# Starting the second expert layer on three tiles after nine of ten row tiles, with late scatters on their own semaphores

## The chip, the cores and the metric

The kernel runs on one core of a Trainium2 chip. A core has a matrix engine (TensorE, PE in the rows), a vector engine (VectorE, DVE), a scalar engine (ScalarE, ACT), GpSimd (POOL) and SyncE (SP), which here only issues DMAs and waits. The engines run their own instruction streams in order and meet at semaphores. The metric is the device time of one execution in microseconds (us), lower is better. The chip grants TensorE a clock at one of two levels, 2.4 or 1.2 GHz; the rows show it as a share, 1.00 or 0.50.

## What is computed

Two layers, each a graph part and a mixture-of-experts part, over 1250 rows of 512 numbers and 20000 edges. What matters here is the end of the second layer, cut from the reference:

```python
    # second graph layer (x: 1250 x 512)
    h = agg * jax.lax.rsqrt(deg_in)[:, None]
    h = h @ W + b
    h = (h - mu) * jax.lax.rsqrt(var + LN_EPS) * gamma + beta
    x = x + gelu(h)
    # second expert layer: one of six experts for each row
    probs = softmax(layernorm(x) @ w_gating)
    gate1 = max(probs);  gate2 = second(probs);  gate1 = gate1 / (gate1 + gate2 + EPS)
    hidden = gelu(layernorm(x) * gamma @ w1[expert])      # 512 -> 256
    x = x + gate1 * (hidden @ w2[expert])                 # 256 -> 512
```

Which expert takes a row is known only when its gating product is there, so rows have to be sorted by expert at run time.

## The kernel before

The 1250 rows are ten row tiles of 125. The end of the program, from 748 us of the profiled execution, runs like this.

**Graph part, per row tile j.** TensorE finishes four column blocks of the last aggregation piece (`aggregate_rest`, L853, ten matmuls of 250 columns each) and multiplies by W (`project(j)`, L880, four matmuls of 512 columns). VectorE adds the bias (`add_bias`, L2040), takes statistics (`hidden_stats`, L2046), centres, shifts (`centre_rows`, L2053; `shift_rows`, L2060), ScalarE does the gelu, VectorE adds it to x (`add_layer`, L2066) and takes statistics again (`layer_stats`, L1540).

**Routing, per row tile i.** TensorE transposes the tile (`turn_unit`, L893), multiplies by the gating weights (`route_unit`, L903) and ranks the rows in their experts (`rank_unit`, L910, one small matmul). VectorE copies the logits (`take_logits1`, L2076), finds the largest and its index (`best_of`, `index_of`, `number_of`), makes the one-hot mask (`mask_of`, L2096) that the ranking needs, and turns ranks into slots (`take_slots`, L2103 to L2106). Running counts pass from tile to tile, so the tiles are ranked in order. ScalarE writes the normalised rows (`unit_rows`) and GpSimd scatters them to their slots in memory (`scatter_unit`, L1454), an area of 1280 slots for each expert. All ten scatters add to one semaphore, `rows1_out`. SyncE meanwhile stores x to `x_d` (L301), from which it is gathered later.

**Hand-over.** After the tenth tile TensorE takes out the counts (L958) and VectorE works out, for 15 tiles of 128 slots, the expert and the first slot (`take_counts`, L1798 to L1814; `slot1_made`). VectorE then scales the logits (L2233, L2235), ScalarE takes their exponential (L1267), VectorE makes the gate of every row (L2238 to L2245; `gate1_made`), and SyncE writes the gates beside the rows in `x_d` (two small DMAs, L301).

**Expert tiles, t = 0 to 14.** SyncE loads a tile from the slots (`load_rows1`, L459); the first three after `slot1_made` and all ten scatters, the others when a buffer is free. Between the third and the fourth load stands the wait for `gate1_made` with the write of the gates. TensorE transposes the rows (`turn_rows1`, L766, ×4), does the hidden product (L759, four matmuls of 256 columns), transposes the hidden rows (`turn_hidden`, L766, ×2) and does the output product (L759, two matmuls of 512 columns). ScalarE moves the transposes (L1272, L1282) and does the gelu (L1277). GpSimd gathers x and the gate of the tile's rows from `x_d` (`gather_kept`, L1492), which needs every store to `x_d` (`x_kept`), the gates among them. VectorE adds gate × product to x (`add_kept`, L2259; `yy_moved`), and GpSimd scatters the result to the output (L1499). `output_product(t)` writes one of two banks and waits for `yy_moved` of tile t - 2.

The order of all these steps on each engine is written out by hand in the source. In the first expert layer the same hand-over exists in two steps already: its first 6 tiles are known after 7 row tiles (`EARLY_TILES`, `EARLY_ROWS`).

Of the kernel before, what the change touches and what calls it, by code (L numbers as in the profile page):

```python
# [39 lines left out]
AHEAD = 3  # L40
E0, H0, K0 = 8, 256, 2
# [5 lines left out]
EARLY_TILES, EARLY_ROWS = 6, 7  # L47
assert K0 * P * EARLY_ROWS - E0 * (TM - 1) > (EARLY_TILES - 1) * TM
assert E == EP * ET and N == P * T and MT0 % LANES == 0
# [40 lines left out]
def gnn_moe_kernel(nc, x, src, dst, L0_gnn_W, L0_ffn_gate_w, L0_ffn_w1, L0_ffn_w2, L0_ffn_w3,  # L90
# [7 lines left out]
    with ExitStack() as ctx:  # L98
# [159 lines left out]
        rows_in = [sem(f"rows_in{k}") for k in range(T)]  # L258
# [14 lines left out]
        SCATTERED0 = [16 * K0 * len(range(k, T, 3)) for k in range(3)]  # L273

        @block.sync
        def _(sp):
# [140 lines left out]
            for t in range(3, MT0 + 2):  # L417
                if t == EARLY_TILES - 1:
                    sp.wait_ge(S("slot_made"), 3)
                    for k in range(3):  # L420
                        sp.wait_ge(rows_out[k], 16 * K0 * len(range(k, T, 3)))
# [14 lines left out]
            sp.wait_ge(rows_in[4], 16 * K0)  # L436
            move(CS_C, counts_d[2 * C * P:N, :].rearrange("(i p) d -> p i d", p=P), S("counts_in2"))
            sp.wait_ge(rows_in[T - 1], 16 * K0)
# [4 lines left out]
            for e in range(E1):  # L443
                sp.dma_start(W1B[:, e, :].rearrange("p (c n) -> p c n", c=C),
                             L1_ffn_w1[e].rearrange("(c p) n -> p c n", c=C)).then_inc(S("w1b_in"), 16)
            sp.wait_ge(S("agg_made"), C * len(AGGREGATED))
# [3 lines left out]
            for i in range(T):  # L450
                sp.wait_ge(S("xn_made"), 2 * T + i + 1)
                move(x_d[P * i:P * i + P, 0:D], X[:, i, :], S("x_kept"))
# [8 lines left out]
            sp.wait_ge(S("rows1_out"), 16 * T)  # L461
            for t in range(3):
                load_rows1(t)
# [9 lines left out]
        def _(pe):  # L473
# [433 lines left out]
            def rank_unit(i):  # L907
# [3 lines left out]
                  .then_inc(S("rank1_made"), 1)  # L911
            project(0)
# [3 lines left out]
            aggregate_rest(0, 0)  # L916
            aggregate_rest(0, 1)
            project(4)
            project(5)
            turn_unit(0)  # L920
            aggregate_rest(0, 2)
            project(6)
            aggregate_rest(0, 3)
            project(7)
            project(8)
            route_unit(0)
            turn_unit(1)
            turn_unit(2)
            route_unit(1)
            rank_unit(0)  # L930
            turn_unit(3)
            route_unit(2)
            rank_unit(1)
            route_unit(3)
            project(9)
            rank_unit(2)
            turn_unit(4)
            turn_unit(5)
            route_unit(4)
            turn_unit(6)  # L940
            rank_unit(3)
            route_unit(5)
            turn_unit(7)
            route_unit(6)
            rank_unit(4)
            route_unit(7)
            rank_unit(5)
            turn_unit(8)
            turn_unit(9)
            rank_unit(6)  # L950
            route_unit(8)
            rank_unit(7)
            route_unit(9)
            rank_unit(8)
            rank_unit(9)

            pe.wait_ge(S("slot1_ready"), T)
            pe.matmul(bank(6, 1, 8), ident[0:126, 125:126], counted[:, T % 2, :], start=True, stop=True)\  # L958
              .then_inc(S("count_made"), 1)
            pe.wait_ge(S("slot1_made"), 1)  # L960
            pe.wait_ge(S("xg_made"), C)
            pe.wait_ge(S("w2b_in"), 16 * E1)
# [3 lines left out]
            def turn_rows1(t):  # L966
                expert1[t] = pe.value_load(owner_i[0:1, t:t + 1], min_val=0, max_val=E1 - 1)
# [4 lines left out]
            def hidden_product(t):  # L972
                pe.wait_ge(S("z_moved"), t + 1)
# [8 lines left out]
            def output_product(t):  # L982
                pe.wait_ge(S("gg_moved"), t + 1)
                above_zero(pe, S("yy_moved"), t - 1)
                product(6 + t % 2, act1T[t % 2], W2B, expert1[t], 2, D).then_inc(S("yy_made"), 1)

            turn_rows1(0)
            for t in range(MT1 + 1):
                if t >= 1:
                    turn_hidden(t - 1)  # L990
# [4 lines left out]
                if t >= 1:  # L995
                    output_product(t - 1)
# [3 lines left out]
        def _(act):  # L1000
# [227 lines left out]
            for n in range(AT_ONCE):  # L1228
                for c in range(C):
                    move_aggregate(n, c)  # L1230
# [1063 lines left out]
```

## Time and profile before

| | |
|---|---|
| median of 3 runs | 912.6 us (912.29 to 912.64) |
| the profiled execution | 913.43 us, its span 911.7 us |
| TensorE busy | 837.7 us, 92% of the span |
| VectorE busy | 568.0 us, 62% |
| ScalarE busy | 375.9 us, 41% |
| GpSimd busy | 205.0 us, 22% |
| mean granted TensorE clock | 0.968 |

The span is the profiled stretch; the execution's own time is 1.73 us more. TensorE is busy nearly throughout, with two holes: one at 663 to 678 us, between the layers, and one at 826 to 838 us, at the hand-over to the second expert layer. This change works on the second.

### The profile page before, as it was taken

How to read it: one execution, taken by the hardware profiler on the slowest of the kernel's cores; microseconds unless marked ns; L12 is line 12 of the kernel's file. 1: busy time of each engine (PE TensorE's matmuls, PEld its weight loads, DVE VectorE, ACT ScalarE, POOL GpSimd, SP SyncE). 2: the span in 40 equal slices, each digit the busy share in tenths (PEclk: the TensorE clock that was granted, in tenths of full speed). 3: DMA queues.
4: the chain of work that ended last, by engine and by line, in shares of the span. 5: the costliest groups of instructions: out<-in, count | busy, mean ns of one | idle time of the engine just before them, and what ended most of it. 6: DMA issues, size and time to landing. Idle time of an engine off the chain costs nothing.

```text
span 911.7 us, 15969 instructions
## 1 busy us (share of the span) xinstructions
PE 837.7 (92%) x5074; PEld 564.6 (62%) x5074; DVE 568.0 (62%) x1880; ACT 375.9 (41%) x680; POOL 205.0 (22%) x376
## 2 busy tenths in 40 slices
PE   6999999999999999999999799999829999993996
PEld 3456555457777777777777667777514446672664
DVE  6389999357777788778777365555544406873111
ACT  1234434456566666566556334343300023341331
POOL 4100000000022012101212512222154502562443
PEclk9999999999999999999999999999969999975999
DMA  9818888796102223110924545554135340364550
GB/s 258 314 28 207 201 209 211 120 341 169 30 25 70 65 76 83 38 43 25 303 72 140 206 123 162 178 166 151 59 87 139 96 146 1 112 196 103 159 171 28
DMA packets 87363, 121.01 MB, mean 133 GB/s; under 512 B 40781, under 2 KB 50157, under 8 KB 87021
## 3 DMA queue, kind: packets, MB, share of 16 engines
q1 hardware_dynamic: 73677, 101.82, 39.1%
q0 software_dynamic: 13600, 18.11, 7.1%
q8 instruction: 46, 0.75, 0.4%
q14 instruction: 40, 0.33, 0.1%
HBM read 65.52 MB, written 57.08 MB: 134 GB/s over the span
## 4 chain that ended last, share of the span: by engine, by line
PE 74%; DVE 13%; DMA 4%; issue 3%; POOL 2%; ACT 2%; SPq 0%; DVEq 0%; POOLq 0%; ACTq 0%
PE ps L759 17%; PE ps L649 10%; PE ps L678 10%; PE ps L853 9%; PE ps L660 8%; PE ps L539 4%; PE ps L880 4%; DVE R_B L1633 4%; PE ps L766 3%; DVE R_B L1632 2%; PE ps L544 2%; DVE R_A L1734 1%; PE ps L489 1%; PE ps L715 1%; DVE R_B L1628 1%
## 5 line engine op out<-in xcount | busy, mean ns | idle before, releaser
L759 PE MATMUL ps<-R_B,R_A 128*128 x612 | 185.9, 445 | 2.9 <-ACT R_A L1272 1.1
L759 PEld LDWEIGHTS ps<-R_B,R_A 128*128 128x128 f32 x612 | 111.4, 193 | 34.8 <-issue 24.8
L1104 ACT ACTIVATE R_A<-R_A,neg_max 125x1250 f32<-125x1250 f32 x80 | 106.6, 1333 | 57.1 <-DVE neg_max L1734 57.1
L1734 DVE CUSTOM_DVE_ANT_0 R_A<-ps,R_B,neg_max 125x417 f32<-125x417 f32 (+1 forms) x160 | 97.7, 649 | 29.0 <-PE ps L649 29.0
L649 PE MATMUL ps<-R_B 64*125 64x417 f32 (+1 forms) x480 | 106.5, 544 | 2.1 <-ACT XN L1046 1.5
L678 PEld LDWEIGHTS ps<-R_W,XN 125*64 125x64 f32 x1600 | 85.3, 136 | 23.9 <-issue 23.8
L660 PE MATMUL ps<-ident,R_A 125*125 125x125 f32 x800 | 98.7, 278 | 0.0
L660 PEld LDWEIGHTS ps<-ident,R_A 125*125 125x125 f32 x800 | 94.9, 188 | 1.5 <-DVE R_W L1741 0.7
L678 PE MATMUL ps<-R_W,XN 125*64 125x125 f32 x1600 | 94.7, 272 | 0.8 <-DVE counted L1791 0.8
L1111 ACT ACTIVATE R_W<-ps 125x500 f32<-125x500 f32 x120 | 66.1, 585 | 51.2 <-PE ps L660 51.2
L1633 DVE TENSOR_SCALAR R_B<-R_B 125x418 bf16<-125x418 uint16 x200 | 77.7, 389 | 0.0
L1734 DVE CUSTOM_DVE_ANT_0 R_A<-ps,R_B 125x417 f32<-125x417 f32 x80 | 44.2, 591 | 45.4 <-PE ps L649 32.1
L539 PE MATMUL ps<-XT,R_W 128*128 128x500 f32 (+1 forms) x192 | 70.9, 513 | 0.7 <-ACT XT L1029 0.7
L766 PEld LDWEIGHTS ps<-ident,R_A 128*128 128x128 f32 x306 | 38.5, 142 | 46.7 <-issue 21.3
L766 PE MATMUL ps<-ident,R_A 128*128 128x128 f32 x306 | 49.2, 277 | 18.7 <-DMA R_A<-slots_d 12.7
L1632 DVE TENSOR_SCALAR R_B<-R_B 125x125 bf16<-125x125 uint16 x200 | 50.8, 254 | 13.3 <-PE ps L489 12.9
L649 PEld LDWEIGHTS ps<-R_B 64*125 64x125 f32 x480 | 39.7, 183 | 29.6 <-issue 21.6
L1741 DVE COPY R_W<-ps 125x500 f32<-125x500 f32 x80 | 53.7, 672 | 3.4 <-PE ps L660 3.3
L489 PE MATMUL ps<-R_B 125*125 125x418 bf16 x200 | 48.6, 351 | 7.2 <-DVE R_B L1633 4.9
L1389 POOL TENSOR_TENSOR rms<-ssum,half_pow 128x1 f32<-128x1 f32 x54 | 29.7, 550 | 109.8 <-DVE ssum L1932 75.7
L539 PEld LDWEIGHTS ps<-XT,R_W 128*128 128x128 f32 x192 | 35.7, 189 | 25.2 <-issue 23.8
L853 PE MATMUL ps<-XT,R_B 125*128 125x500 f32 (+1 forms) x96 | 36.7, 538 | 15.3 <-DVE R_B L2012 15.3
(274 smaller groups left out, 1118.4 us busy)
## 6 DMA issues: line engine op xcount, KB each, us to landing
slots_d<-R_B SPq DMA_DIRECT2D x9, 2322.0 KB, 12.3
R_B<-in_L_ffn_w_dram SPq DMA_DIRECT2D x28, 512.0 KB, 7.1
R_A<-slots_d SPq DMA_DIRECT2D x27, 256.0 KB, 2.9
slots_d<-R_A SPq DMA_DIRECT2D x27, 256.0 KB, 2.6
counts_d<-R_A SPq DMA_DIRECT2D x10, 546.9 KB
logs_d<-R_B SPq DMA_DIRECT2D x10, 546.9 KB
R_B<-logs_d SPq DMA_DIRECT2D x10, 546.9 KB
R_B<-counts_d SPq DMA_DIRECT2D x10, 546.9 KB
```

Source lines behind the costliest of these rows:

```text
L539: ins = pe.matmul(b[:, 0:z - a], Wqkv[:, c, w:w + 128], XT[:, c, a:z], start=c == 0, stop=c == C - 1)
L649: pe.matmul(bank(2 * h + g % 2, P, z - a), QT[r:r + DH, i, j, :], KT[r:r + DH, j, a:z], start=True, stop=True).then_inc(S("s_made"), 1)
L660: ins = pe.transpose(bank(4 + n % 3, P, P, k * P), SC[u % 2][h][:, kt * P:kt * P + P], ident[0:P, 0:P])
L678: ins = pe.matmul(ps[r:r + DH, 512 * 7:512 * 7 + P], XN[:, kt, (2 * j + h) * DH:(2 * j + h) * DH + DH], PT[u % 2][:, T * h + kt, :], start ...
L759: ins = pe.matmul(bank(b, TM, width), lhs[:, c * TM:c * TM + TM], flat[:, bass.ds(e * (n * width) + c * width, width)], start=c == 0, stop ...
L766: ins = pe.transpose(bank(b, 128, TM, c * TM), source[:, c * 128:c * 128 + 128], ident[:, :])
L853: return pe.matmul(bank(b, 128, z - a), HS[i][:, c * 128:c * 128 + 128], counts_of[i][:, a:z], start=i == 0, stop=i == T - 1)
L1104: act.activation(SC[u % 2][h], SC[u % 2][h], ACT.Exp, bias=neg_max[:, 2 * (u % 2) + h:2 * (u % 2) + h + 1], scale=-1.0, accum_out=den[:, 2 ...
L1111: act.activation(PT[u % 2][:, 4 * b:4 * b + 4, :], bank(4 + ring_at(u, b) % 3, P, 4 * P).rearrange("p (i n) -> p i n", n=P), ACT.Copy).the ...
L1632: dve.tensor_scalar(oh_dst[:, slot, :], iota_dst, win[:, 0, w:w + 1], None, ALU.is_equal)
L1633: return dve.tensor_scalar(hot_of[:, slot, 0:width], iota_src[:, 0:width], win[:, 1, w:w + 1], win[:, 2, w:w + 1], ALU.is_equal, ALU.mult)
L1734: dve.tensor_tensor_reduce(SC[u % 2][h][:, a:z], bank(2 * h + g % 2, P, z - a), LNB[i % 2][:, a:z], -1.0, least if t else 3.0e38, ALU.add, ...
```

## The change

- **Early units.** Nine row tiles fill at least three expert tiles whatever the routing is (1125 rows less 6 × 127 is over two tiles of 128). After row tile 9 of 10 TensorE takes the counts out once more (`take_out_units(0)`), VectorE works out expert and first slot of three full tiles (`early_units`, `early_owners`), and the first three loads wait for that and for nine scatters alone. The rest, 12 tiles, follows after the tenth tile (`rest_counts`, `rest_owners`, `rest_bases`), with about twice as many one-partition VectorE instructions in all.
- **Semaphores.** Scatters of late row tiles (the tenth here, the last three in the first expert layer) add to `row_moved[i]` instead of the shared ones.
- **Stores.** SyncE stores row tiles 0 to 3 of x ahead of the W2 loads (`KEPT_AHEAD`).
- **Orders.** The written-out orders of the stage are new on all engines. The first three expert tiles have their own order on TensorE and ScalarE: the exponential, which stood ahead of the expert tiles on ScalarE, stands behind the gelu of the third.
- In the first expert layer only semaphores and names change; which work waits for which is as before.

The core of the diff:

```diff
@@ SyncE
             sp.wait_ge(S("slot1_made"), 1)
-            sp.wait_ge(S("rows1_out"), 16 * T)
-            for t in range(3):
+            sp.wait_ge(S("rows1_out"), 16 * EARLY_UNIT_ROWS)
+            for t in range(EARLY_UNITS):
+                load_rows1(t)
+            sp.wait_ge(S("slot1_made"), 3)
+            for i in range(EARLY_UNIT_ROWS, T):
+                sp.wait_ge(row_moved[i], gathered(i) + 16)
+            for t in range(EARLY_UNITS, 3):
                 load_rows1(t)
             sp.wait_ge(S("gate1_made"), 1)
             move(x_d.rearrange("(i p) w -> p i w", p=P)[:, :, D:WIDE], gate_rows, S("x_kept"))
...
@@ TensorE
+            def take_out_units(k):
+
+                n = T if k else EARLY_UNIT_ROWS
+                pe.wait_ge(S("slot1_ready"), n)
+                pe.matmul(bank(7, 1, 8, 8) if k else bank(1, 1, 8), ident[0:126, 125:126], counted[:, n % 2, :], start=True, stop=True)\
+                  .then_inc(S("count_made"), 1)
...
             turn_rows1(0)
-            for t in range(MT1 + 1):
-                if t >= 1:
-                    turn_hidden(t - 1)
+            turn_rows1(1)
+            hidden_product(0)
+            hidden_product(1)
+            turn_hidden(0)
+            turn_rows1(2)
+            turn_hidden(1)
+            output_product(0)
+            hidden_product(2)
+            output_product(1)
+            turn_rows1(3)
+            for t in range(3, MT1 + 1):
+                turn_hidden(t - 1)
...
@@ ScalarE
-            act.wait_ge(S("g1_step"), 1)
-            act.activation(logits[:, :, 0:E1], logits[:, :, 0:E1], ACT.Exp).then_inc(S("g1_exp"), 1)
...
             move_rows1(0)
+            move_rows1(1)
+            gelu1(0)
+            gelu1(1)
+            move_hidden(0)
+            move_rows1(2)
+            move_hidden(1)
+            gelu1(2)
+            act.wait_ge(S("g1_step"), 1)
+            act.activation(logits[:, :, 0:E1], logits[:, :, 0:E1], ACT.Exp).then_inc(S("g1_exp"), 1)
+            move_rows1(3)
...
@@ VectorE
+            def early_units():
+
+                dve.wait_ge(S("count_made"), 3)
+                link(dve.tensor_scalar(cnt_i[0:1, :], bank(1, 1, 8), 0.0, None, ALU.add))
+                early_counts()
...
             mask_of(9)
+            early_owners(EARLY_UNITS, owner[:, 0:EARLY_UNITS, :], S("slot1_made"))
             take_slots(9)
-            take_counts(MT1, E1, S("slot1_made"), 3)
+            early_done(EARLY_UNITS)
+            rest_counts(bank(7, 1, 8, 8), 4, S("slot1_made"))
+            rest_owners(EARLY_UNITS, MT1, E1)
+            rest_bases(EARLY_UNITS, MT1, S("slot1_made"))
```

**TensorE around the last projection.** Before, `project(9)` (125x512, L880) stands after the ranking of tile 1 (126x8, L910) and two routings (125x6, L903):

```order
L903 MATMUL ps<-gate_w,R_A 125x6 x4
L910 MATMUL ps<-counted,before 126x8
L903 MATMUL ps<-gate_w,R_A 125x6 x4
L880 MATMUL ps<-R_W,R_A 125x512 x4
L910 MATMUL ps<-counted,before 126x8
L893 MATMUL ps<-ident,X 128x125 x8
```

After, the same place (`project(9)` is L902, ranking L932, routing L925, transposing L915):

```order
L915 MATMUL ps<-ident,X 128x125 x4
L932 MATMUL ps<-counted,before 126x8
L925 MATMUL ps<-gate_w,R_A 125x6 x4
L932 MATMUL ps<-counted,before 126x8
L902 MATMUL ps<-R_W,R_A 125x512 x4
L932 MATMUL ps<-counted,before 126x8
L925 MATMUL ps<-gate_w,R_A 125x6 x4
```

The last projection moved behind the rankings of tiles 2 and 3, with all transposes up to tile 6 ahead of it.

**ScalarE at the hand-over.** Before, the exponential (L1267, R_A<-R_A) and the two loads of function tables around it stand ahead of the hidden rows of any tile:

```order
L1267 ACT_TABLE_LOAD
L1267 ACTIVATE R_A<-R_A 125x10x6 [waits g1_step]
L1272 ACTIVATE R_A<-ps 128x512 [waits z_turned]
L1277 ACT_TABLE_LOAD
L1277 ACTIVATE R_A<-ps 128x256 [waits hh_made]
```

After (L1313 moves the rows' transposes, L1318 is the gelu, L1323 moves the hidden transposes, L1334 is the exponential):

```order
L1313 ACTIVATE R_A<-ps 128x512 [waits z_turned] x2
L1318 ACTIVATE R_A<-ps 128x256 [waits hh_made] x2
L1323 ACTIVATE R_A<-ps 128x256 [waits gg_turned]
L1313 ACTIVATE R_A<-ps 128x512 [waits hh_made,z_turned]
L1323 ACTIVATE R_A<-ps 128x256 [waits gg_turned]
L1318 ACTIVATE R_A<-ps 128x256 [waits gg_turned,hh_made]
L1334 ACT_TABLE_LOAD
L1334 ACTIVATE R_A<-R_A 125x10x6 [waits g1_step]
L1313 ACTIVATE R_A<-ps 128x512 [waits hh_made,z_turned]
L1323 ACTIVATE R_A<-ps 128x256 [waits yy_made,gg_turned]
L1318 ACT_TABLE_LOAD [waits gg_turned]
```

The exponential went from ahead of tile 0 to behind the gelu of tile 2.

**SyncE behind the third load.** After, the write of the gates (L312) and the fourth load (L475, L476) stand like this; before, the rows are the same but for the first, which waits for `gate1_made` alone:

```order
L476 DMA R_A<-slots_d 128x516
L312 DMA x_d<-R_A 112x10x4 [waits gate1_made,row_moved9,slot1_made]
L312 DMA x_d<-R_A 13x10x4
L475 TENSOR_LOAD base_i [waits token_made,z_turned]
L475 ISA x2
L476 ISA
```

The fourth load's place behind the wait for the gates did not move; what moved is when the gates are made.

## Rows read from the trace of the kernel before

**Rows 1.** The page: the chain that ended last, by engine.

```profile
PE 74%; DVE 13%; DMA 4%; issue 3%; POOL 2%; ACT 2%; SPq 0%; DVEq 0%; POOLq 0%; ACTq 0%
```

**Rows 2.** The chain of waits, 748 to 856 us: start us, us, what.

```profile
748.08 13.73 PE ps L880 x32
761.81 8.44 PE ps L853 x40
...
802.50 5.23 PE ps L880 x8
...
826.52 7.77 DMA slots_d<-R_B,slot
...
835.25 2.63 DMA R_A<-slots_d
...
837.93 1.13 PE ps L766 x4
...
839.82 3.75 PE ps L759 x8
...
854.97 0.44 PE ps L766 x4
855.41 1.72 PE ps L759 x4
```

**Rows 3.** Windows: span, then PE, PEld, DVE, ACT, POOL busy (instructions), PEclk, DMA share, GB/s.

```profile
665.00:670.00 5.00, 0.00 (x0) 0.00 (x0) 0.00 (x0) 0.00 (x0) 3.73 (x3) 0.59 0.24 50
802.00:804.00 2.00, 2.00 (x7) 1.08 (x7) 1.90 (x8) 0.63 (x1) 0.25 (x2) 0.61 1.07 378
...
808.00:810.00 2.00, 1.75 (x17) 1.52 (x15) 1.90 (x10) 1.63 (x3) 1.19 (x1) 1.00 0.38 112
...
842.00:844.00 2.00, 2.00 (x8) 1.30 (x7) 0.00 (x0) 0.38 (x1) 0.56 (x1) 0.65 0.53 115
```

**Rows 4.** Timeline of VectorE, 808 to 832 us: start us, us, line, operation.

```profile
809.43 0.68 DVE L2046 BATCH_NORM_STATS2 stats<-R_B 125x6 f32<-125x512 f32 x1
...
810.42 0.74 DVE L2053 SCALAR_TENSOR_TENSOR R_B<-R_B,mv 125x512 f32<-125x512 f32 x1
811.09 0.16 DVE L2081 MAX8 R_A<-R_A 125x8 f32<-125x8 f32 x1
...
823.41 0.17 DVE L2103 COPY counted<-ps 126x8 f32<-126x8 f32 x1 [0.15 <-PE ps L910]
...
823.82 0.15 DVE L2106 CAST slot<-slot_f 125x1 int32<-125x1 f32 x1
...
827.72 0.16 DVE L1809 TENSOR_SCALAR owner_f<-owner_f 1x15 f32<-1x15 f32 x1
...
831.47 0.18 DVE L2245 COPY R_A<-gates 125x40 f32<-125x40 f32 x1
```

**Rows 5.** One line's answer: scatters of the routing, L1454, issue to landing.

```profile
DMA to landing us min/median/max: 5.2/6.1/7.8
```

**Rows 6.** Timeline, 829 to 849 us: ScalarE, SyncE, GpSimd, VectorE.

```profile
829.62 0.25 ACT L1267 ACTIVATE R_A<-R_A 125x60 f32<-125x60 f32 x1 [8.12 <-DVE R_A L2235]
...
839.70 1.28 ACT L1277 ACT_TABLE_LOAD   x1
...
837.91 1.10 SPq L301 DMA_DIRECT2D x_d<-R_A  x2
...
843.44 1.06 POOL L1492 DMA_INDIRECT R_A<-x_d,token  x1 [15.73 <-DMA x_d<-R_A]
...
839.39 0.15 DVE L2251 COPY token<-R_A 128x1 int32<-128x1 int32 x1 [1.33 <-DMA R_A<-slots_d]
...
848.96 0.75 DVE L2259 SCALAR_TENSOR_TENSOR R_A<-ps,R_A 128x512 f32<-128x512 f32 x1 [8.17 <-PE ps L759]
```

**Rows 7.** One line's answer: gathers from x_d, L1492, issue to landing.

```profile
DMA to landing us min/median/max: 2.1/3.5/5.0
```

**Rows 8.** One line's answer: loads of expert tiles, L459, issue to landing.

```profile
DMA to landing us min/median/max: 2.5/2.9/4.6
```

More of the change, by code:

```diff
@@ L40 @@
 AHEAD = 3
+KEPT_AHEAD = 4
 E0, H0, K0 = 8, 256, 2
@@ L257, in gnn_moe_kernel @@
         s = {n: sem(n) for n in names.split()}
-        rows_in = [sem(f"rows_in{k}") for k in range(T)]
+        row_moved = [sem(f"row_moved{k}") for k in range(T)]
         def S(n):
@@ L445, in _, with keep_rows @@
                              L1_ffn_w1[e].rearrange("(c p) n -> p c n", c=C)).then_inc(S("w1b_in"), 16)
+            def keep_rows(i):
+                sp.wait_ge(S("xn_made"), 2 * T + i + 1)
+                move(x_d[P * i:P * i + P, 0:D], X[:, i, :], S("x_kept"))
+            for i in range(KEPT_AHEAD):
+                keep_rows(i)
             sp.wait_ge(S("agg_made"), C * len(AGGREGATED))
@@ L449, in _ @@
                              L1_ffn_w2[e].rearrange("(c p) n -> p c n", c=2)).then_inc(S("w2b_in"), 16)
-            for i in range(T):
-                sp.wait_ge(S("xn_made"), 2 * T + i + 1)
-                move(x_d[P * i:P * i + P, 0:D], X[:, i, :], S("x_kept"))
+            for i in range(KEPT_AHEAD, T):
+                keep_rows(i)
             def load_rows1(t):
@@ L952, in _ @@
             rank_unit(7)
+            rank_unit(8)
+            turn_unit(9)
+            take_out_units(0)
             route_unit(9)
-            rank_unit(8)
             rank_unit(9)
[L957 to L962, printed above, removed]
+            take_out_units(1)
             expert1 = {}
             def turn_rows1(t):
+                if t == EARLY_UNITS:
+                    pe.wait_ge(S("slot1_made"), 3)
                 expert1[t] = pe.value_load(owner_i[0:1, t:t + 1], min_val=0, max_val=E1 - 1)
@@ new lines, in rest_bases @@
+            def rest_bases(first, tiles, made):
+                rest, base = owner[:, 0:tiles - first, :], base_f[:, first:tiles]
+                link(dve.tensor_tensor(rest, rest, cnt[0:1, 3:4, :].to_broadcast([1, tiles - first, 8]), ALU.mult))
+                link(dve.tensor_reduce(base, rest, X_AXIS, ALU.add))
+                link(dve.scalar_tensor_tensor(base, iotaT[:, 0:tiles - first], taken[:, 0:1], base, ALU.add, ALU.add))
+                dve.tensor_scalar(base_i[:, first:tiles], base, float(TM), None, ALU.mult).then_inc(made, 1)
@@ L2174, in _ @@
+            layer_stats(6)
+            take_slots(0)
+            mask_of(1)
+            add_bias(8)
+            take_logits1(2)
+            hidden_stats(8)
+            best_of(2)
+            centre_rows(8)
+            take_logits1(3)
+            take_slots(1)
+            best_of(3)
+            add_layer(7)
             index_of(2)
             number_of(2)
+            take_logits1(4)
+            mask_of(2)
+            best_of(4)
+            index_of(3)
+            index_of(4)
+            number_of(3)
@@ L2176, in _ @@
+            take_slots(2)
+            mask_of(3)
+            shift_rows(8)
+            take_logits1(5)
+            best_of(5)
+            take_slots(3)
+            index_of(5)
+            number_of(4)
             layer_stats(7)
-            take_slots(1)
-            mask_of(2)
+            mask_of(4)
             add_layer(8)
             layer_stats(8)
-            take_logits1(3)
-            take_slots(2)
-            best_of(3)
             add_bias(9)
-            index_of(3)
-            number_of(3)
+            number_of(5)
@@ L2221, in _ @@
             number_of(8)
+            mask_of(8)
+            add_layer(9)
+            take_slots(8)
+            layer_stats(9)
+            early_units()
             take_logits1(9)
-            mask_of(8)
             best_of(9)
```

325 lines of the change are left out of this document (142 added, 183 removed).

## Prediction, made before the changed kernel was run

> **What bounds the kernel now.** I read the page's chain first [rows 1]: three quarters of the end is TensorE, so only holes in TensorE's work, or work added to it, move the time. The chain of waits from 748 us [rows 2] shows the one hole this change aims at: the tenth scatter is issued at 826.52, lands at 834.30, the first load is issued at 835.25 and lands 2.63 later, and TensorE starts tile 0 at 837.93. From there two dates serve as marks: T0 = 837.93, the first transpose of tile 0, and the start of the output product of tile 2 at 855.41, which is T0 + 17.5. Behind that mark the order is the same in both kernels, so its shift is the shift of the end. The windows [rows 3] give the clock: in 665 to 670, where TensorE had nothing to do, it averaged 0.59, so it fell from 1.00 to 0.50 in that window, and after the restart at 837.93 it came back only within 842 to 844 (0.65). So a restart from a hole of several microseconds runs about 5 us at 1.2 GHz, and a transpose of four blocks takes 1.13 instead of 0.44 there [rows 2].
>
> **Part 1: when the ninth scatter lands.** In program order TensorE now does four blocks of the aggregation, nine projections, three transposes and two routings up to the end of `project(8)`. A projection is 13.73 / 4 = 3.43, a block 8.44 / 2 = 4.22 [rows 2], a transpose or routing about 0.44: 30.9 + 16.9 + 2.2 = 50.0, so 748.1 + 50.0 = 798.1. The operations are the old ones moved, and VectorE's bias additions are ahead of each projection's bank, so I see no new wait here. Until `project(9)` TensorE waits for masks, so VectorE sets the pace. From `take_slots(0)` at 799.0 to `mask_of(3)` it has three wide operations (0.66 from start to start), one statistics pair (0.82), 14 narrow ones (0.16) and three `take_slots` (0.56: 823.41 to 823.97) [rows 4], and 0.4 of wait: 2.0 + 0.8 + 2.2 + 1.7 + 0.4 = 7.1. With the ranking that follows, `project(9)` starts at 806.4. Before it started at 802.50 and took 5.23 [rows 2], its first half in a window with the clock at 0.61 [rows 3]. TensorE has less to do in the microseconds ahead of it now, so at least as slow: 5.2 taken, bounds 3.43 (full clock) and 6.9 (half), end at 811.6. Moving it costs nothing by itself, but it holds all that is behind it on TensorE, `rank_unit(4)` first. From there VectorE needs until `take_slots(8)`: four wide (2.6), a statistics pair (0.8), 17 narrow (2.9), five `take_slots` (2.8) and about 1.0 of waits for rankings, 10.2 in all, so the ninth slots are ready at 821.8 against 823.97 before [rows 4]. GpSimd is not busy with roots then (`logit_roots` moved behind the tenth scatter), so the scatter leaves at once; 6.1 to land, bounds 5.2 and 7.8 [rows 5], gives 827.9. SyncE adds what it added before, 834.30 to 837.93 = 3.6 [rows 2]. Tile 0 starts at T0' = 831.5, **6.4 earlier**.
>
> The early bases must be there too: statistics of tile 9 (0.8) after 821.8, six one-partition operations of 0.2 (0.16 and a short gap [rows 4]), five narrow ones of the tenth tile and seven more of 0.2 end at 826.2, 1.7 ahead of the landing. Hidden, unless the scatter lands faster than any row shows. The later ones (about 22 × 0.2 = 4.4 behind the tenth slots) end at 831.4, the tenth scatter (issued 827.5) lands at 833.6: both far ahead of the fourth tile, whose wait is part 2. The four stores brought forward (8 DMAs on SyncE's queue) leave as their rows are ready, ahead of the W2 loads, whose first user is output product 0 some 40 us later; the semaphores of the late scatters change names, not waits: nothing for both.
>
> The Trainium skill (DMA: Bandwidth & Descriptors, Anatomy of one DMA) fits a GpSimd-issued DMA as 2.0 us plus its bytes over 436 GB/s, an estimate of 2.6 us for these 258 KB. The rows show 5.2 at least, so the trace disagrees; by the page the bases would decide, tile 0 would start 1.7 earlier and my sum would be 915.0 instead of 916.7.
>
> **Part 2: the gates come late.** This is the term that decides. Before, the exponential ran at 829.62 and the gates were ready at 831.65 [rows 4, 6], 6 us ahead of tile 0, in the shadow of the scatters. Now the exponential stands on ScalarE behind the gelu of tile 2, and that needs TensorE's hidden product of tile 2. Counted from T0': transpose 1.13 (slow clock), move 0.60, transpose of tile 1 (its load lands 1.5 after the first, token at 839.39 [rows 6]) to 2.6, hidden product 0 3.7 (3.75 as before) to 6.3, hidden product 1 at full clock 1.72 (as many columns as the output product [rows 2]) to 8.0, two transposes of hidden rows and one of tile 2 (0.22, 0.22, 0.44) to 9.0, output product 0 1.72 to 10.8, hidden product 2 to 12.5, output product 1 to 14.3. The gelu of tile 2 ends at 13.0, a table load 1.28 and the exponential 0.25 [rows 6] bring 14.6, and the gates take 829.87 to 831.65 = 1.8 [rows 4, 6]: **16.4**.
>
> Two things hang on the gates.
> - SyncE's fourth load is queued behind them. Two small writes 1.1 [rows 6], 0.9 to read the base and issue (as 834.30 to 835.25 [rows 2]), 2.5 to 4.6 to land [rows 8], taken near the upper end, 3.9, because the small writes are ahead of it: 22.3. TensorE, whose next instruction is the transpose of tile 3, has nothing from 14.3 to 22.3, a **new hole of 8 us**, and even the ready transpose of tile 2's hidden rows is queued behind. It restarts at 1.2 GHz: transpose 0.9, move 0.7, hidden product 3.5, transpose of tile 4 0.6: 28.0. At full clock it would be 25.8.
> - GpSimd's gathers need every store to `x_d`. From SyncE's issue to GpSimd's start 837.91 to 843.44 = 5.5 [rows 6], gather 3.5 [rows 7], `add_kept(0)` 0.8 [rows 6]: 16.4 + 9.8 = 26.2. The output product of tile 2 waits for that too.
>
> So the mark is at T0' + **28.0**, bounds 26.2 and about 30 (load at 4.6, the small writes slower beside it), where it was T0 + 17.5. That is 10.5 lost against 6.4 won: **+4.1 us**. No other work covers the hole: all that TensorE has behind it in order is tile 3. From the mark on all loads and gathers are ahead again and a tile takes 2 × 1.72 + 0.44 + 0.22 = 4.1 as before.
>
> A second rule bears on this term. The Trainium skill (ScalarE: Activation LUTs, What ACT_TABLE_LOAD costs) charges a switch of tables 1.28 us and a drain of 1.38. The row shows the 1.28 and none of the drain; by the page the gates would come at 17.8 and the sum be 918.1.
>
> **The sum.** The profiled execution took 913.43, its span 911.7. 913.43 + 4.1 = 917.5; the median of the three runs shown is 0.8 lower, so **916.7** for the median.
>
> **The rivals.**
> - *The clock stays up.* If TensorE keeps 2.4 GHz through the rankings and the new start, `project(9)` takes 3.43 (1.8 saved), the scatter may land in 5.2 (0.9), transpose and first product of tile 0 save 2.7, and the restart behind the hole is bounded by the gathers (26.2 less 2.7 = 23.5). The mark is at 828.8 + 23.5 = 852.3 against 855.41: 3.1 faster, **909.5**. It gets onto this side once more than 4.1 + 1.8 is saved. For it: the clock was 1.00 in 808 to 810 with small matmuls only [rows 3]. Against it: 0.61 in 802 to 804 [rows 3], and TensorE has nothing to do for some 4 us ahead of tile 0. With half of these savings the time comes out within 0.2%, about **912.6**.
> - *The early start is not early.* If the ranking chain is as long as the old one, or the ninth scatter is queued behind stores of x and lands late, tile 0 starts at 837 and the late gates cost their whole 10.5: up to **923**. For it: VectorE's new order has five `take_slots` behind one projection. Against it: the counted work.
> - *The change doesn't do what it says.* The hand-over of three tiles might be there but the loads wait for the tenth scatter anyway. The order of SyncE speaks against that; it would give the same 923.
>
> **How the numbers follow.** Forecast (+2 to +7, 914.5 to 920): 0.60. Early start lost, whichever way (above 920): 0.12. Half the savings, within 0.2%: 0.14. The clock stays up: 0.14. A difference of 0.2%, 1.8 us, is about what a measurement of this kernel can tell from no change. So faster 0.14, same 0.14, slower 0.72. The range: down to 910.5, which takes in most of the two lighter cases (scatter 5.2 and `project(9)` 3.43 with the gates late as forecast give 914.0), and up to 922.0, which takes in 6.9, 7.8 and 30 together (+1.7, +1.7, +2 = 922.1) and leaves out the worst of the lost start.
>
> **What would show it.** Right if in the new profile (1) the first transpose of expert tiles starts near 831, (2) the exponential runs about 13 to 15 us behind it with a table load just ahead, (3) a TensorE hole of 6 to 9 us lies between the second output product and the fourth tile's transpose, released by a load, with a clock of 0.50 behind it, and (4) the first `add_kept` starts near T0' + 25. Wrong if the hole is short because the gates came earlier than 16 us after T0', or if tile 0 starts before 829 or after 834; then the terms of part 1 (projection 9, the 10.2 of VectorE, the landing) are to be compared one by one.

## The result and the profile after

The changed kernel takes **917.9 us** (median of 4 runs, 917.11 to 918.59) against 912.62 for the kernel before (912.29 to 912.81): 1.0054 times as long, 95% interval 1.0035 to 1.0073, 5.3 us more. Beside other kernels it was measured once more: 918.54 against 912.9, ratio 1.0061 (1.0044 to 1.0078). The forecast was 916.7 in a range of 910.5 to 922.0, slower with 0.72.

The profiled execution took 917.11 us, its span 915.4. The page of the changed kernel gives the chain by engine, as [rows 1] for before. It says nothing of the cause; TensorE's share is the same, "issue" has 1% more and DMA 1% less:

```profile
PE 74%; DVE 13%; issue 4%; DMA 3%; ACT 2%; POOL 2%; SPq 0%; DVEq 0%; POOLq 0%; ACTq 0%
```

The chain of waits of the changed kernel, 793 to 836 us (start us, us, what), answers to [rows 2]: the projections of row tiles 8 and 9, the ninth scatter with its landing, SyncE's reading of a base, the load of the first expert tile, and the first transpose of expert tiles, at T0' = 833.65.

```profile
793.18 3.44 PE ps L902 x8
...
805.60 5.88 PE ps L902 x8
...
821.11 6.96 DMA slots_d<-R_B,slot
...
828.14 0.45 SPq L475
...
829.02 4.58 DMA R_A<-slots_d
833.65 1.97 PE ps L788 x8
```

GpSimd's timeline in the same stretch: five scatters. The first four leave one behind another, 1.5 to 2.0 us apart; the last comes after a pause.

```profile
816.09 1.23 POOL L1504 DMA_INDIRECT slots_d<-R_W,slot  x1 [0.28 <-issue]
817.63 1.19 POOL L1504 DMA_INDIRECT slots_d<-R_W,slot  x1 [0.30 <-issue]
819.12 1.68 POOL L1504 DMA_INDIRECT slots_d<-R_B,slot  x1 [0.30 <-issue]
821.11 1.19 POOL L1504 DMA_INDIRECT slots_d<-R_B,slot  x1 [0.30 <-issue]
...
826.91 1.27 POOL L1504 DMA_INDIRECT slots_d<-R_B,slot  x1 [3.34 <-DVE slot L2130]
```

Then the hole. The timeline of the changed kernel, 841 to 861 us, TensorE, ScalarE, SyncE, GpSimd and VectorE one after another, beside [rows 6] of before:

```profile
841.20 5.42 PE L781 MATMUL ps<-R_B,R_A 128*128 x16
853.54 1.54 PE L788 MATMUL ps<-ident,R_A 128*128 128x128 f32 x6 [6.92 <-DMA R_A<-slots_d]
855.43 3.22 PE L781 MATMUL ps<-R_B,R_A 128*128 x8 [0.35 <-ACT R_A L1313]
...
858.92 1.88 PE L781 MATMUL ps<-R_B,R_A 128*128 x4
...
844.94 0.38 ACT L1318 ACTIVATE R_A<-ps 128x256 f32<-128x256 f32 x1 [3.12 <-PE ps L781]
845.34 1.28 ACT L1334 ACT_TABLE_LOAD   x1
846.64 0.26 ACT L1334 ACTIVATE R_A<-R_A 125x60 f32<-125x60 f32 x1
...
848.76 1.00 SPq L312 DMA_DIRECT2D x_d<-R_A  x2
850.75 2.73 SPq L476 DMA_DIRECT2D R_A<-slots_d  x3
...
852.61 1.16 POOL L1543 DMA_INDIRECT R_A<-x_d,token  x1 [22.07 <-DMA x_d<-R_A]
...
857.30 0.75 DVE L2294 SCALAR_TENSOR_TENSOR R_A<-ps,R_A 128x512 f32<-128x512 f32 x1 [8.44 <-DMA R_A<-x_d,token]
```

In the order of cause and effect: the exponential (L1334) runs at 846.64, 13.0 behind T0', with a table load just ahead; the gates' two small writes leave at 848.76, the fourth tile's load at 850.75, and TensorE, which had nothing since 846.6, starts its transpose at 853.54. GpSimd, idle for 22 us, starts its gathers only after the same writes. The output product of tile 2, the mark of the prediction, starts at 858.92 = T0' + 25.3.

The windows of the changed kernel (columns as in [rows 3]; PEclk is the third figure from the end) show the clock: at 0.50, that is 1.2 GHz, for the larger part of projection 9, which runs from 805.60 to 811.48, though TensorE was busy throughout, and back at full speed for its end (0.96 in 810 to 812); and at 0.50 again behind the hole, where the fourth tile begins.

```profile
798.00:800.00 2.00, 2.00 (x18) 1.85 (x18) 1.97 (x6) 2.00 (x4) 1.75 (x3) 0.98 1.01 352
...
808.00:810.00 2.00, 2.00 (x4) 0.80 (x3) 0.83 (x2) 0.81 (x1) 1.58 (x5) 0.50 0.56 149
810.00:812.00 2.00, 2.00 (x12) 1.26 (x10) 0.49 (x1) 0.81 (x1) 0.26 (x1) 0.96 0.66 179
...
836.00:838.00 2.00, 2.00 (x7) 1.60 (x7) 0.00 (x0) 0.25 (x1) 0.00 (x0) 0.63 0.03 8
...
848.00:852.00 4.00, 0.00 (x0) 0.00 (x0) 0.75 (x7) 0.00 (x0) 0.00 (x0) 0.89 0.23 10
...
854.00:856.00 2.00, 1.65 (x7) 1.18 (x6) 0.00 (x0) 1.29 (x3) 1.63 (x2) 0.50 0.90 270
```

### The profile page after: what moved, and what is told of

The parts are those of the page before. It is cut to its first block, busy times and chain, and to the rows that moved or that the text cites. A ratio compares the mean times of both kernels' runs of the same rounds, so it can differ in the third digit from the quotient of the medians.

```text
span 915.4 us, 15995 instructions
## 1 busy us (share of the span) xinstructions
PE 838.0 (92%) x5076; PEld 566.4 (62%) x5076; DVE 569.2 (62%) x1897; ACT 376.4 (41%) x680; POOL 205.4 (22%) x376
## 4 chain that ended last, share of the span: by engine, by line
PE 74%; DVE 13%; issue 4%; DMA 3%; ACT 2%; POOL 2%; SPq 0%; DVEq 0%; POOLq 0%; ACTq 0%
PE ps L781 17%; PE ps L671 10%; PE ps L700 10%; PE ps L875 9%; PE ps L682 8%; PE ps L561 4%; PE ps L902 4%; DVE R_B L1684 4%; PE ps L788 4%; DVE R_B L1683 2%; PE ps L566 2%; DVE R_A L1785 1%; PE ps L511 1%; DMA R_A<-slots_d 1%; PE ps L737 1%
## 5 line engine op out<-in xcount | busy, mean ns | idle before, releaser
L561 PE MATMUL ps<-XT,R_W 128*128 128x500 f32 (+1 forms) x192 | 73.4, 529 | 0.6 <-ACT XT L1071 0.6
L1439 POOL TENSOR_TENSOR rms<-ssum,half_pow 128x1 f32<-128x1 f32 x54 | 29.7, 550 | 109.6 <-DVE ssum L1954 74.6
L561 PEld LDWEIGHTS ps<-XT,R_W 128*128 128x128 f32 x192 | 37.2, 197 | 25.6 <-issue 23.7
```

Of the source, the lines that this page charges most:

```text
L561: ins = pe.matmul(b[:, 0:z - a], Wqkv[:, c, w:w + 128], XT[:, c, a:z], start=c == 0, stop=c == C - 1)
```

## A scale for all kernels of this study

Two executions don't reach the stage at the same moment: TensorE ended the main aggregation, the last operation that has the same place in both programs, at 748.08 in the profile of before and at 745.84 in that of after, though nothing ahead of it was changed but names and semaphores. Over 14 traces that date lies between 745.84 and 748.93, about as much as the times of one kernel spread. So I cut each span in four, all by TensorE's timeline: up to that date (start), from there to the first transpose of expert tiles (T0), from there to the output product of tile 2 (mark), and the rest. The rest is 56.41 to 56.50 us in every kernel but e2 (56.80) and e3 (58.64, told below), so within one execution mark minus start carries the effect of an edit. Each line of the table is one execution: its last column, with the rest added for e2 and e3, lies within 1.2 us of the difference of the medians in every kernel but e8, where it is 2.4 off. (By the timeline the mark of before is 855.24; the chain of [rows 2] has it 0.17 later.)

| kernel | start | T0 − start | mark − T0 | mark − start | against before |
|---|---|---|---|---|---|
| before | 748.08 | 89.85 | 17.31 | 107.16 | |
| after | 745.84 | 87.81 | 25.27 | 113.08 | +5.9 |
| f0, after again | 747.97 | 87.31 | 25.58 | 112.89 | +5.7 |
| e1, exponential first | 748.61 | 87.53 | 16.64 | 104.17 | −3.0 |
| f1, the same | 746.55 | 87.17 | 16.88 | 104.05 | −3.1 |
| e2, before with it late | 746.38 | 89.72 | 28.50 | 118.22 | +11.1 |
| e3, loads freed | 748.93 | 87.99 | 23.14 | 111.13 | +4.0 (rest +2.2) |
| e4, tenth scatter held | 746.48 | 85.92 | 20.97 | 106.89 | −0.3 |
| e5, start held | 747.27 | 90.04 | 17.12 | 107.16 | 0.0 |
| f5, the same | 748.92 | 90.15 | 17.02 | 107.17 | 0.0 |
| e7, projection 9 early | 746.57 | 89.21 | 17.50 | 106.71 | −0.5 |
| e8, plain loop | 748.29 | 86.38 | 17.78 | 104.16 | −3.0 |
| e9, roots first | 748.26 | 85.86 | 17.44 | 103.30 | −3.9 |
| f9, the same | 746.56 | 86.40 | 17.17 | 103.57 | −3.6 |

## Experiments on the late gates

**Exponential first (e1, f1).** The changed kernel with one operation of ScalarE put back where before had it:

```diff
+            act.wait_ge(S("g1_step"), 1)
+            act.activation(logits[:, :, 0:E1], ..., ACT.Exp).then_inc(S("g1_exp"), 1)
             move_rows1(0)
             move_rows1(1)
...
             gelu1(2)
-            act.wait_ge(S("g1_step"), 1)
-            act.activation(logits[:, :, 0:E1], ..., ACT.Exp).then_inc(S("g1_exp"), 1)
```

> The changed kernel with one edit: the exponential of the logits goes back on ScalarE to where it was, ahead of the rows of any expert tile. Everything else, the early start and the new orders too, stays. Late-gates theory: the gates are ready about 833, before tile 0 is transposed; the hole between the second output product and the fourth tile's transpose (6.9 us) is gone, the output product of tile 2 starts 15.9 us behind the transpose of tile 0 instead of 25.4, and the time falls by 9.6 us from 917.9 to about 908.3, below the kernel before. Rival (the hole comes from the new order of the first three tiles or from the wait for the tenth scatter, the gates only pass by): less than 2 us, about 916.

Measured: 909.75 against 912.77, ratio 0.9955 (0.9939 to 0.9970). Again, beside the three other kernels of the last group:

> The kernel e1 once more, beside the three others of this call on one chip, since its first measurement stood on another chip than e5 and e9. Theory A (the early start is worth about 2 us): 910 to 911, 1 to 2 us under the kernel with the held start and 0 to 1.5 above the one with the tenth scatter held behind the roots. Rival B (its first measurement is the true distance): 908.5 to 909.8, 3 us or more under the held start.

909.66 against 912.9, ratio 0.9962 (0.9947 to 0.9978): rival B's number, 3 us or more under the held start of f5 below. Both are faster than both kernels of this case. The time of e1 fell by 8.2 and not by the 9.6 of its late-gates theory, and the rival's 916 is ruled out. Timeline of f1, ScalarE, SyncE, GpSimd, TensorE:

```profile
831.83 0.25 ACT L1326 ACTIVATE R_A<-R_A 125x60 f32<-125x60 f32 x1 [5.42 <-DVE R_A L2270]
...
836.59 5.91 SPq L476 DMA_DIRECT2D R_A<-slots_d  x3
...
838.12 1.16 POOL L1543 DMA_INDIRECT R_A<-x_d,token  x1 [6.88 <-DMA x_d<-R_A]
...
841.71 5.42 PE L781 MATMUL ps<-R_B,R_A 128*128 x16
846.97 0.82 PE L788 MATMUL ps<-ident,R_A 128*128 128x128 f32 x6
848.34 1.99 PE L781 MATMUL ps<-R_B,R_A 128*128 x8 [0.56 <-ACT R_A L1313]
```

The exponential runs 1.9 us ahead of the first transpose, the fourth load leaves at 836.59, and TensorE goes from the second output product straight to the fourth tile: the hole of 6.92 is gone. **The changed kernel itself once more (f0)**, on the same chip:

> The changed kernel itself once more on the same chip: 917 to 919, 7 to 8.5 us above f1, which is the price of the exponential behind the gelu of tile 2 as predicted for the loop (10.5 us forecast, 8.0 read from the profile).

918.54. So one operation of 0.25 us, standing 15 us later on ScalarE, costs 918.54 − 909.66 = **8.9 us**; the table gives 112.89 − 104.05 = 8.8. That is a little more than the 7 to 8.5 expected.

**The same delay alone (e2).** The kernel before, with its exponential behind the gelu of tile 2 and nothing else changed:

```diff
                 if t < MT1:
                     gelu1(t)
+                if t == 2:
+                    act.wait_ge(S("g1_step"), 1)
+                    act.activation(logits[:, :, 0:E1], ..., ACT.Exp).then_inc(S("g1_exp"), 1)
```

> The kernel before with one edit: the exponential moved behind the gelu of tile 2 on ScalarE. Late-gates theory: the fourth load and the gathers wait here too; the gates come near 854.6 instead of 831.7, the fourth tile is there near 859.5, the output product of tile 2 starts near 867 instead of 855.4, and the time is about 924 (922 to 926). Rival (the late gates are covered, the loss comes with the early start): 912.6, no change.

923.58, ratio 1.0120 (1.0078 to 1.0162), as the late-gates theory had it. Timeline of e2, TensorE, then ScalarE:

```profile
847.26 1.89 PE L759 MATMUL ps<-R_B,R_A 128*128 x8
857.79 1.12 PE L766 MATMUL ps<-ident,R_A 128*128 128x128 f32 x4 [8.64 <-DMA R_A<-slots_d]
858.70 3.62 PE L759 MATMUL ps<-R_B,R_A 128*128 x4
...
849.60 1.28 ACT L1290 ACT_TABLE_LOAD   x1
850.89 0.26 ACT L1290 ACTIVATE R_A<-R_A 125x60 f32<-125x60 f32 x1
```

The delay alone is enough for the hole; in the plain order it is longer (8.64), because the transpose of tile 3 stands ahead of the output product of tile 1, which then runs at half clock (3.62 instead of 1.88). The reordered loop of the changed kernel therefore gave 11.06 − 8.84 = 2.2 us of the damage back.

**Which of the two followers holds TensorE (e3).** The changed kernel with the fourth and fifth load ahead of SyncE's wait for the gates, and the first three `take_tokens` ahead of the gates on VectorE; the gates as late as before:

```diff
-            for t in range(EARLY_UNITS, 3):
-                load_rows1(t)
+            load_rows1(3)
+            load_rows1(4)
             sp.wait_ge(S("gate1_made"), 1)
...
-            for t in range(3, MT1):
+            for t in range(5, MT1):
```

> The changed kernel with the gates as late as they are, but the fourth and fifth loads no longer behind them on SyncE, and the tokens of the first three tiles taken ahead of the gates on VectorE. It tells apart the two things that hang on the gates. If the load alone makes the hole, the output product of tile 2 starts 16 us behind tile 0 and the time is about 909. If the gathers hold it as well (my theory: the first addition ended 24.4 us behind tile 0), TensorE goes on to the hidden product of tile 3, then stands idle some 8 us, and the output product of tile 2 starts at 24.4 with the clock at 0.50 behind it: 917 to 920, no gain.

919.21, ratio 1.0064 (1.0046 to 1.0083): nothing gained, as my theory had it. Timeline of e3, TensorE, GpSimd, VectorE:

```profile
852.78 0.60 PE L788 MATMUL ps<-ident,R_A 128*128 128x128 f32 x4
860.06 3.77 PE L781 MATMUL ps<-R_B,R_A 128*128 x4 [6.69 <-DVE R_A L2295]
...
855.49 1.16 POOL L1543 DMA_INDIRECT R_A<-x_d,token  x1 [21.90 <-DMA x_d<-R_A]
...
859.07 0.75 DVE L2295 SCALAR_TENSOR_TENSOR R_A<-ps,R_A 128x512 f32<-128x512 f32 x1 [7.27 <-DMA R_A<-x_d,token]
```

The load's hole is gone, and one of 6.69 opens a product further on: the output product of tile 2 needs the bank that `add_kept(0)` frees, and that waits for the gathers. It starts at T0' + 23.1, earlier than 25.3, but at half clock, 3.77 instead of 1.88, which the rest of the span shows as +2.2. So the gathers alone are enough for the loss. That the late load would be enough by itself is read from the changed kernel, where the transpose of tile 3 is released by it and `add_kept(0)` was done at 858.05, ahead of the mark at 858.92; no run freed the gathers and left the load late.

## Experiments on the early start

**The first loads held (e5, f5).** e1, in which SyncE's first three loads wait for the tenth scatter too:

```diff
             sp.wait_ge(S("rows1_out"), 16 * EARLY_UNIT_ROWS)
+            for i in range(EARLY_UNIT_ROWS, T):
+                sp.wait_ge(row_moved[i], gathered(i) + 16)
```

> The kernel with the exponential ahead of the expert tiles, in which SyncE's first three loads wait for the tenth scatter as well: the early start is taken away and the new order of the tiles stays. Theory A (the early start is worth only about 2 us, since the first load beside the tenth scatter takes 4.6 instead of 2.6 and the chain to the ninth slots is longer than I worked out): tenth scatter lands near 832.5 to 833, first load issued near 833.7, alone and so 2.6 long, tile 0 near 836.5 against 836.1 with the early start; 910 to 911.5, that is within 0.2% of the kernel without this edit. Rival B (the early start is worth the 6.4 us that the prediction gave it): 914 to 916.

912.1 against 912.2, ratio 1.0005 (0.9994 to 1.0015). And beside f1:

> The kernel e5 once more (exponential first, the first three loads wait for the tenth scatter). Theory A: 911.5 to 912.5, within 0.2% of the kernel before, since without the early start nothing of the new order is left that shortens TensorE's path.

913.58, ratio 1.0007 (0.9994 to 1.0020). In e5 both numbers missed, theory A's 910 to 911.5 and rival B's 914 to 916: it stands in between. In f5 the time is within 0.2% of before, as theory A said, though 1.1 above its 912.5. Without the early start the new order is worth nothing against before (107.16 and 107.17 against 107.16), so the early start is worth 107.17 − 104.05 = **3.1 us** (the medians of f5 and f1, each known to about 1.4 us against before, differ by 3.9). From f5's chain of waits, the tenth scatter, issued with nothing behind which to queue, and from its timeline the first transpose and the mark:

```profile
829.97 5.49 DMA slots_d<-R_B,slot
...
839.07 1.12 PE L790 MATMUL ps<-ident,R_A 128*128 128x128 f32 x4 [9.43 <-DMA R_A<-slots_d]
...
856.09 1.88 PE L783 MATMUL ps<-R_B,R_A 128*128 x4
```

**The tenth scatter held (e4).** e1, with one wait on GpSimd ahead of `scatter_unit(9)`, for the landing of the first tile:

```diff
             unit_root(9)
+            pool.wait_ge(xs_in[0], 16 * G0 + 16)
             scatter_unit(9)
             logit_roots()
```

> The kernel with the exponential first, and the tenth scatter held back on GpSimd until the first expert tile has landed. It tests whether the first load took 4.6 us instead of 2.6 because the tenth scatter was in flight beside it. Contention theory: the first load lands in 2.6 to 3.1, tile 0 starts 1.5 to 2 us earlier, and some of it is kept: 0.5 to 1.5 us faster than the kernel with the exponential first alone, about 907.3. Rival (the load is slow for another reason, such as reading rows just written): the first load takes 4.6 still and the time is the same or up to 2 us more, since the writes of the gates now wait for a later tenth scatter.

912.97, ratio 0.9997 (0.9981 to 1.0012): no gain but 3.2 us more than e1, and for neither theory's reason. On the load the contention theory was right, 2.71 with the tenth scatter held. Timeline of e4, TensorE, ScalarE, GpSimd:

```profile
832.40 1.11 PE L788 MATMUL ps<-ident,R_A 128*128 128x128 f32 x4 [5.12 <-DMA R_A<-slots_d]
...
838.08 5.45 PE L781 MATMUL ps<-R_B,R_A 128*128 x16 [2.99 <-ACT R_A L1313]
...
837.10 0.26 ACT L1326 ACTIVATE R_A<-R_A 125x60 f32<-125x60 f32 x1 [10.69 <-DVE R_A L2271]
...
834.56 1.99 POOL L1492 TENSOR_TENSOR out_max<-out_max,half_pow 125x10 f32<-125x10 f32 x1
```

T0 did come earlier, 85.92 behind the start instead of 87.2 to 87.5. But `logit_roots` is queued behind the held scatter on GpSimd, the exponential needs it, and tile 0's move is queued behind the exponential on ScalarE: 2.99 us of wait ahead of the first hidden product. I had named the queue of the held instruction nowhere in the expectation.

**Roots first (e9, f9).** The same with `logit_roots()` ahead of the wait.

> The kernel with the exponential ahead of the expert tiles, with the tenth scatter held until the first tile has landed as in e4, but with GpSimd's roots for the gates ahead of that wait, so that they no longer hold the exponential and with it ScalarE. Theory (a load beside the tenth scatter takes 4.6 instead of 2.7, and e4 lost this gain again because the roots stood behind the held scatter): first load issued 829.5 and landed near 832.3, tile 0 near 832.4, its move not held; the fourth load then waits for the tenth scatter, 832.4 + 7 = 839.5, + 3.6 = 843, while TensorE has work until T0' + 14 = 846: no hole; 906 to 908. Rival (the held scatter slows the loads of tiles 1 and 2 instead, or the fourth tile comes late): 909 to 911, no better than without the edit.

909.51 against 912.2, ratio 0.9971 (0.9960 to 0.9982): the rival's 909 to 911, not the theory's 906 to 908. And beside f1:

> The kernel e9 once more (exponential first, tenth scatter held until the first tile has landed, roots ahead of it). Theory A (the load is 2 us shorter when no scatter moves beside it): 908.5 to 910, 0.5 to 2 us under f1. Rival B (the load of tile 0 gains 2 us and the loop gives most of it back, since the first hidden product then waits for ScalarE's exponential): equal to f1 within 0.5 us.

909.51, ratio 0.9962 (0.9949 to 0.9974), against f1's 909.66: rival B, no difference that can be measured. f9's chain of waits and its windows, the last three lines; f1 and f9 have the same start (746.55, 746.56), so their times can be laid side by side:

```profile
821.81 7.33 DMA slots_d<-R_B,slot
...
834.00:836.00 2.00, 1.74 (x7) 1.58 (x7) 0.31 (x2) 1.11 (x2) 0.80 (x1) 0.50 0.45 131
836.00:838.00 2.00, 2.00 (x6) 1.55 (x6) 0.00 (x0) 1.37 (x2) 0.00 (x0) 0.50 0.31 87
838.00:840.00 2.00, 2.00 (x11) 1.74 (x10) 0.00 (x0) 0.38 (x1) 0.00 (x0) 0.96 0.07 20
```

The two windows of f1:

```profile
836.00:838.00 2.00, 2.00 (x7) 1.64 (x6) 0.12 (x1) 1.58 (x2) 0.00 (x0) 0.50 0.26 32
838.00:840.00 2.00, 2.00 (x11) 1.77 (x10) 0.00 (x0) 0.69 (x2) 1.58 (x2) 0.96 0.76 221
```

f9 starts tile 0 at 832.96, f1 at 833.72, 0.76 later, and the clock comes back in the same 2 us, with the same 0.50 and 0.96, in both. What f9 does earlier it does at 1.2 GHz (the first pair of hidden products takes 5.05 instead of 4.61), so 0.3 of the 0.76 is lost again. Rival B's reason, a first hidden product that waits for ScalarE's exponential, isn't what the trace shows: the exponential ended at 831.62, ahead of tile 0. The ninth scatter took 7.33 in f9 with the tenth held until 833.49: its long landing is not the tenth's doing.

**Projection 9 early (e7).** e1 with `project(9)` moved from behind `rank_unit(3)` to behind `route_unit(3)`.

> The kernel with the exponential ahead of the expert tiles, with the projection of row tile 9 moved ahead on TensorE from behind the ranking of tile 3 to behind the routing of tile 3. In the trace it took 6.1 us at half clock and held the ranking of tile 4 and all behind it for 5 of these. Theory A (VectorE and GpSimd are the bound of the slot chain too: the ninth slots come 1 to 2 us earlier, but GpSimd issues the scatters at 1.5 us each, so the ninth leaves hardly earlier): within 1 us of the kernel without this edit, 909 to 910. Rival B (TensorE's place of this projection sets the chain): ninth slots 3 us earlier, ninth scatter lands near 826, 907 to 908.

911.92, ratio 1.0002 (0.9988 to 1.0015). Rival B fell, and the kernel came out above theory A too: the ninth scatter left 76.3 us behind the start instead of 75.2. TensorE's routing products between 815 and 820 us took 1.74 and 1.84 us each where e1's took 0.97 to 1.02, with the granted clock at 0.50 from 812 to 822 (in f1 it was 1.00 from 812 to 816). The time that the projection had cost in one place the clock took in another. Both products are on e7's chain of waits:

```profile
815.64 1.84 PE ps L925 x8
...
817.91 1.74 PE ps L925 x8
```

**Plain loop (e8).** e1 with TensorE's and ScalarE's expert tiles in the loop of the kernel before.

> The kernel with the exponential ahead of the expert tiles, with the expert tiles on TensorE and ScalarE in the plain loop of the kernel before (hidden rows, next hidden product, next transpose, output product), so that only the hand-over of three tiles is left of the new order. Theory A (the unrolled order of the first three tiles brings next to nothing: both orders give TensorE the same work, and the mark was at T0 + 17.5 in the plain order and T0 + 16.6 in the new one): 909.5 to 911, 0 to 1 us above the kernel without this edit. Rival B (the unrolled order matters, since the second tile's products fill the wait for ScalarE's gelu of the first): 912 or more. In the plain order the first output product stands ahead of the wait for later bases only by one place, which costs nothing here.

911.61 against 912.2, ratio 0.9993 (0.9983 to 1.0003), between theory A's 909.5 to 911 and rival B's 912. Within the stage the trace shows no loss (104.16), but its projection 9 took 5.08 instead of 6.08, which hides one; from T0 to the mark the plain order takes 0.9 to 1.1 more than e1 and f1. The median lies some 2 us above what the stage explains (0.6 under before, not 3.0), and no e1 ran beside it, so how much the new order of the tiles brings with early gates, 1 or 2 us, stays open.

## Why the prediction was right, step by step

The sign, the cause and the place were right. Two terms were each too large, the early start by 4.4 (6.4 forecast, 2.0 measured) and the loss in the loop by 2.5 (10.5, 8.0), and their errors partly cancel, which is luck: +4.1 forecast, +5.9 and +5.7 in the traces, +5.3 and +5.6 in the medians. The sum on the profiled execution, 917.5, hit 917.11 only because that execution reached the stage 2.2 us early, luck again.

- **The signs.** Tile 0 was to start near 831 and not after 834. It started at 833.65, inside only by those 2.2 us: counted from the start as in before it is 835.9, and f0 has 835.28. The gates came 15.0 behind T0', ahead of the 16 that the prediction gave as another sign of being wrong, yet the hole was 6.92, in its 6 to 9. The exponential at 13.0, the load that releases the hole and the clock of 0.50 behind it came as said; the first `add_kept` came at 23.7 against 25. So part 2 held and part 1 didn't hold in size.
- **Projections 8 and 9.** Projection 8 ended at 796.6, 50.8 behind the start (50.0 forecast; a routing takes 0.77 to 0.87 and not the 0.44 that I gave it); projection 9 began 59.8 behind it (58.3) and took 5.88 (5.2, bounds 3.43 and 6.9). "At least as slow" was the right side, but the reason was wrong: TensorE didn't wait for masks with less to do, it was busy 1.95 to 2.00 of every 2 us ahead of it, the chain of waits there is TensorE's own, and the clock was 0.50 from 800 to 810.
- **Ninth scatter issued.** Forecast 73.7 behind the start, measured 75.3. VectorE's stretch behind projection 9, for which I took 10.2 (its terms add up to 10.1, and 17 narrow operations of 0.16 are 2.7, not 2.9), took 8.9, and this gave back 1.3 of the 2.1 lost before it. The slots were ready at 820.39, 74.6 behind the start; "the scatter leaves at once" left out 0.7. f5's tenth, with GpSimd free, needs 0.56 from the slots too, and here GpSimd was issuing the scatter of tile 7 until 820.80: the chain of waits from 813.10 on goes over GpSimd's scatters and roots.
- **Landing.** I took the median, 6.1, of [rows 5]; it took 6.96, and 7.56, 7.43 and 7.33 in f0, f1 and f9. The nearer row stood in [rows 2]: the last scatter of a row of four issued 1.5 us apart took 7.77. The lone tenth one of f5 took 5.49. The rival's other cause, stores of x, was not tried: in the changed kernel the last store of x is issued from 819.8 to 822.5, beside this scatter, while before's 7.77 had none beside it, so how much the store adds stays open. The Trainium skill (DMA: Bandwidth & Descriptors, Anatomy of one DMA) would give 2.6 for these bytes, an estimate; even the lone scatter took twice that, so its 915.0 fell.
- **Load of tile 0, with 2.0 the largest error in the changed kernel's profile.** From the landing to T0' I took before's 3.6; it was 5.6 in after and 4.6 and 4.5 in f0 and f1. In all seven traces with the tenth scatter in flight it was 4.5 to 6.5; in the seven without, e4, e9 and f9 with the tenth held among them, 3.6 to 3.8. Together with the rest of part 1: T0' came 2.0 (after) and 2.5 us (f0) earlier, not 6.4.
- **The gates.** Ready at T0' + 15.0, not 16.4: the second output product follows the first and the hidden product of tile 2 without the gaps that I had left in (5.42 for the three). The Trainium skill (ScalarE: Activation LUTs, What ACT_TABLE_LOAD costs) adds a drain of 1.38 to the 1.28; here the load starts 0.02 behind the gelu and the exponential 0.02 behind the load, so the trace shows none and its 918.1 fell as a reason, though the time came out near it.
- **From the gates to the mark.** The fourth load took 2.75, not 3.9; the transpose came at T0' + 19.9 (22.3), the mark at 25.3 (28.0). The loop lost 8.0, not 10.5. The structure held: a hole of 6.92, released by the load, and e3 shows the gathers as the second bound.
- **Hidden parts.** The early bases were there at 825.9, 2.2 ahead of the landing; the rest of the span behind the mark was the same to 0.1 us. The stores brought forward and the renamed semaphores were not tried by themselves; 107.16 in e5 bounds them, with the whole new order of row tiles, at nothing in sum.
- **Rivals.** "The clock stays up" fell: 0.50 from 800 to 810 and at T0'. "The early start is not early" was two thirds true, for the reasons above. "The change doesn't do what it says" fell: the first load leaves at 829.02, before the tenth scatter, issued at 826.91, lands 6.1 later.

## What to carry to other kernels

An operation of a quarter of a microsecond can cost nine when it is queued on an in-order engine behind work that it doesn't need: for each instruction of a new order, ask what is ahead of it on its engine and who waits for its semaphore, and move the small one first. An early start is worth only what is left of it: here the long landing and the first load beside the next scatter took 2.9 us (after) and 2.4 (f0) of the 6.4 forecast, and in f9 a start at 1.2 GHz took 0.3 of 0.76. Take the landing from a row with the same neighbours, not from a median. Compare two profiles from the last point that both share, not from their ends.

## What the runs showed of the hardware that I had not expected

- A scatter of 258 KB landed in 5.49 us alone. In a row issued 1.5 to 2.0 us apart the landings grew, 5.1, 5.9, 6.8, 7.0 in the changed kernel; the ninth took 6.3 to 7.6 over all traces of the new order, and before's tenth 7.77 (7.83 in e2). The row is not the only thing: the first scatter of all, at 798.10 with none ahead of it, took 8.1 while the DMA engines' share was 0.9 to 1.1.
- A load of a tile (258 KB) took 2.6 to 2.8 without a scatter in flight. Beside one it took 4.58 in the changed kernel, 5.47 in e3 and 4.54 in e7; in f0 and f1 the load itself was short, 2.7 and 2.8, but SyncE's reading of the base took 1.30 and 1.09 instead of 0.45. Why it falls on one or the other stays open.
- TensorE fell to 1.2 GHz from 800 us on though it was busy 1.95 to 2.00 us of every 2 with routings, transposes and rankings; and with the same start it came back in the same 2 us for two restarts 0.76 us apart.
- The same instruction is reached at different dates in two executions of one program: 745.84 and 747.97 (after, f0), 748.61 and 746.55 (e1, f1). The cause lies in the first 746 us and was not looked for.
